# Row terms of the attention scores computed once as a row, from high and low parts, and added to the turned maxima

## What is computed

```python
cq = jnp.einsum('bcd,bqd,d->bcq', c, q, w_cq) + b_cq
s = (c @ w_c + b_c)[:, :, None] + (q @ w_q + b_q)[:, None, :] + cq
a = jax.nn.softmax(s, axis=2)
c2q_att = jnp.einsum('bcq,bqd->bcd', a, q)
b_att = jax.nn.softmax(jnp.max(s, axis=2), axis=1)
q2c_att = jnp.einsum('bc,bcd->bd', b_att, c)[:, None, :]
x = jnp.concatenate([c, c2q_att, c * c2q_att, c * q2c_att], axis=-1)
z = x @ W_l.T + b_l
```

## Time and profile before

| | us |
|---|---|
| median of three runs (430.25 to 432.04) | 431.75 |
| the profiled execution, its own time | 431.75 |
| its span, first to last instruction | 430.1 |
| PE busy in the span | 411.1 |
| DVE busy | 332.1 |
| ACT busy | 214.2 |

### The profile page before, as it was taken

The page is one execution under the profiler, slowest core; times in us unless marked ns, Lnnn a source line. Parts: engine busy times, 40 slices in busy tenths (PEclk is TensorE's granted clock), DMA queues, the critical chain, the costliest instruction groups (busy, mean ns, idle before and its releaser), DMA issues.

```text
span 430.1 us, 8272 instructions
## 1 busy us (share of the span) xinstructions
PE 411.1 (96%) x3090; PEld 313.3 (73%) x3090; DVE 332.1 (77%) x618; ACT 214.2 (50%) x369; POOL 60.1 (14%) x80
## 2 busy tenths in 40 slices
PE   1999999999999999999999979999999999999995
PEld 1566566688898899985568746787777778777783
DVE  4759689966169782449957989899988888988766
ACT  4345225131465343131516333698788887778410
POOL 2130000000432120111102801000000000000152
PEclk9999999999999999999989999999999999999999
DMA  8999697999951450019123579899999999994662
GB/s 291 393 377 360 251 427 307 382 409 407 419 195 26 130 216 2 2 29 414 52 94 154 202 223 366 313 346 375 387 392 379 360 373 381 357 359 197 219 197 98
DMA packets 25006, 116.74 MB, mean 271 GB/s; under 512 B 3286, under 2 KB 3302, under 8 KB 18448
## 3 DMA queue, kind: packets, MB, share of 16 engines
q1 hardware_dynamic: 12448, 92.28, 55.7%
q10 hardware_dynamic: 10448, 19.15, 11.7%
q0 software_dynamic: 2080, 4.90, 3.6%
HBM read 94.04 MB, written 21.23 MB: 268 GB/s over the span
## 4 chain that ended last, share of the span: by engine, by line
PE 82%; DVE 8%; ACT 3%; DMA 2%; POOL 2%; issue 2%; ACTq 0%; DVEq 0%
PE banks L2013 5%; PE banks L2014 5%; PE banks L2015 5%; PE banks L2046 4%; PE banks L1623 4%; PE banks L1627 4%; PE banks L2057 3%; PE banks L2056 3%; PE banks L2055 3%; PE banks L1624 3%; PE banks L1610 3%; PE banks L1664 3%; PE banks L1591 3%; PE banks L1858 3%; PE banks L1734 3%; PE banks L1744 3%
## 5 line engine op out<-in xcount | busy, mean ns | idle before, releaser
L1374 DVE TENSOR_TENSOR w_lo<-w,w_hi 128x1024 fp32r<-128x1024 f32 x48 | 55.5, 1218 | 0.0
L662 ACT ACTIVATE w_hi<-w 128x1024 fp32r<-128x1024 f32 x48 | 47.4, 1095 | 2.4 <-DMA w<-in_w 2.4
L747 ACT ACTIVATE A<-banks,b_sb 128x128 f32<-128x128 f32 x112 | 30.5, 384 | 25.9 <-PE banks L2026 16.4
L2013 PE MATMUL banks<-w_hi,cT_r 128*128 128x512 f32 x100 | 40.1, 401 | 0.0
L2015 PE MATMUL banks<-w_hi,cT_r 128*128 128x512 f32 x100 | 39.0, 390 | 0.0
L2014 PE MATMUL banks<-w_lo,cT_r 128*128 128x512 f32 x100 | 39.0, 390 | 0.0
L1477 DVE COPY A<-banks 128x512 f32<-128x512 f32 x28 | 18.0, 685 | 10.2 <-PE banks L2015 10.2
L858 POOL TENSOR_TENSOR A<-A,hrec 128x1024 f32<-128x1024 f32 x8 | 17.1, 2138 | 61.0 <-DVE hrec L1192 61.0
L900 POOL DMA_DIRECT2D b_sb<-in_b1T x12 | 6.5, 543 | 135.8 <-ACT A L747 120.2
L1623 PE MATMUL banks<-w_lo,A2r 128*128 128x512 f32 x52 | 22.7, 436 | 1.5 <-ACT A2r L529 1.3
L1183 DVE TENSOR_REDUCE hmax<-banks 128x16 f32<-128x1024 f32 x8 | 9.8, 1221 | 18.2 <-PE banks L1809 18.2
(11 more groups left out here) (353 smaller groups left out, 1037.9 us busy)
## 6 DMA issues: line engine op xcount, KB each, us to landing
w<-in_w SPq DMA_DIRECT2D x24, 2048.0 KB, 7.8
rows_dram<-A ACTq DMA_DIRECT2D x1, 14592.0 KB, 50.6
A<-in_ctxT SPq DMA_DIRECT2D x8, 1024.0 KB, 8.8
A<-in_ctx SPq DMA_DIRECT2D x8, 1024.0 KB, 8.6
w<-in_w SPq DMA_DIRECT2D x5, 1024.0 KB, 7.9
w<-in_wlT SPq DMA_DIRECT2D x3, 1024.0 KB, 15.2
wqkv<-in_wqkvT SPq DMA_DIRECT2D x1, 3072.0 KB, 14.9
w<-in_convT SPq DMA_DIRECT2D x1, 3072.0 KB, 13.4
```

The lines of the kernel that those rows point to most:

```text
L662: nc.scalar.activation(w1_hi[:, u, k * F:(k + 1) * F], w1[:, u, k * F:(k + 1) * F], ACT.Copy).then_inc(hi_ready, 1)
L747: ins = nc.scalar.activation(hT[:, u, f, :], HT[f // 4][:, tile(f % 4)], ACT.Gelu, bias=b1_sb[:, u, f:f + 1])
L1374: nc.vector.tensor_tensor(w1_lo[:, u, part], w1[:, u, part], w1_hi[:, u, part].bitcast(F32), ALU.subtract).then_inc(lo_ready, 1)
L2013: mm(HP[u][c][:, :], xr[:, 0, u, k, :], high[:, at], start=(i == 0), stop=False)
```

## The change

The four `row_terms` go. In their place one `row_terms()` has the vector `wc` as stationary operand, and the parts of all four tiles stream past it: for each k three fp32r products, high with high, high with low parts of the tokens, and the vector's low part with the high parts. That is done for tile 0 (128 columns) and for tiles 1 to 3 together (384 columns), 24 instructions in all, and the result is a row in `MI[0:2, 0:512]`. The vector is held twice, so that the stationary operand has two columns. `split_wc` makes its high and low parts on DVE. `take_token_rows` adds the biases and puts the row in SBUF, on storage that another tensor uses later, since `MI` takes other results from then on.

`token_sums` goes. PE now turns `nmax` itself (`turn_maxima`), and DVE's `token_maxima` subtracts the turned row from the stored one in one operation where it had a copy.

The order moves with it. On PE `project_c(2)` stands ahead of `turn_weights(0)`, the new `row_terms()` behind it, `turn_maxima(0)` behind `attend(0)` and `turn_shares(0)` behind `project_c(3)`. On DVE `low_part(0, 3)` moves ahead of `widen(1)`. For the other tiles `turn_maxima(n)` stands where the turn of `msum` stood.

```diff
-        msum = sb("msum", [P, NT])
...
+        wc_hi, wc_lo = sb("wc_hi", [P, KT, 2], F32R), sb("wc_lo", [P, KT, 2], F32R)
...
-        wtmp = sb("wtmp", [P, NT, E]); wselT = sb("wselT", [ROWS3, NT, P], F32R)
-
+        wtmp = sb("wtmp", [P, NT, E]); wselT_f, wselT = overlaid("wselT_f", "wselT", [ROWS3, NT, P])
+
+        token_rows = wselT_f[0:1, :, :].rearrange("o t (j s) -> o t j s", j=2)
...
-            def token_sums(n):
-
-
-                dve.wait_ge(r_psum, n + 1)
-                dve.wait_ge(nmax_ready, n + 1)
-                link(nc.vector.scalar_tensor_tensor(msum[:, n:n + 1], nmax[:, n:n + 1], -1.0, MI[:, 0:1],
-                                                    ALU.mult, ALU.add))
-                nc.vector.tensor_scalar(msum[:, n:n + 1], msum[:, n:n + 1], bsum[:, 0:1], None, ALU.add) \
-                    .then_inc(m_ready, 1)
+            def split_wc():
+
+                dve.wait_ge(score_params_in, 16 * SCORE_PARAMS)
+                twice = wc[:, :].unsqueeze(2).to_broadcast([P, KT, 2])
+                link(nc.vector.tensor_copy(wc_hi[:, :, :], twice))
+                nc.vector.tensor_tensor(wc_lo[:, :, :], twice, wc_hi[:, :, :].bitcast(F32), ALU.subtract).then_inc(wc_parts, 1)
+
+            def take_token_rows():
+
+                dve.wait_ge(r_psum, 1)
+                nc.vector.tensor_scalar(token_rows, MI[0:1, :].rearrange("o (t j s) -> o t j s", t=NT, j=2),
+                                        bsum[0:1, 0:1], None, ALU.add).then_inc(m_ready, 1)
             def token_maxima(n):
                 dve.wait_ge(mT_psum, n + 1)
-                link(nc.vector.tensor_copy(mT[:, :, :], MI[0:1, P:2 * P].rearrange("p (j s) -> p j s", j=2)))
+                dve.wait_ge(m_ready, 1)
+                link(nc.vector.scalar_tensor_tensor(mT[:, :, :], MI[0:1, P:2 * P].rearrange("p (j s) -> p j s", j=2),
+                                                    -1.0, token_rows[:, n], ALU.mult, ALU.add))
...
-            dve.wait_ge(score_params_in, 16 * SCORE_PARAMS)
+            split_wc()
             link(nc.vector.tensor_reduce(bsum[:, :], scal[:, :], AX.X, ALU.add))
-            token_sums(0)
             low_part(0, 2)
+            low_part(0, 3)
             widen(1)
+            take_token_rows()
             token_maxima(0)
-            low_part(0, 3)
             token_shares(0)
...
-            token_sums(1)
...
-                    token_sums(n + 1)
...
-            def row_terms(n):
-
-                if n:
-                    pe.wait_ge(q2c_taken, n)
-                else:
-                    pe.wait_ge(score_params_in, 16 * SCORE_PARAMS)
-                for k in range(KT):
-                    ins = mm(MI[:, 0:1], cT[:, k, tile(n)], wc[:, k:k + 1], start=(k == 0), stop=(k == KT - 1))
+            def row_terms():
+
+                pe.wait_ge(wc_parts, 1)
+                pe.wait_ge(part_high[0], NT)
+                pe.wait_ge(part_low[0], NT)
+                ahead_parts = parts_ahead.rearrange("p t a k n -> p a k t n")
+                for at, high, low in ((tile(0), parts[:, 0, 0], parts[:, 0, 1]),
+                                      (slice(P, N), ahead_parts[:, 0], ahead_parts[:, 1])):
+                    for k in range(KT):
+                        mm(MI[0:2, at], wc_hi[:, k, :], high[:, k], start=(k == 0), stop=False)
+                        mm(MI[0:2, at], wc_hi[:, k, :], low[:, k], start=False, stop=False)
+                        ins = mm(MI[0:2, at], wc_lo[:, k, :], high[:, k], start=False, stop=(k == KT - 1))
                 ins.then_inc(r_psum, 1)
             def turn_weights(n):
...
                 if n:
                     pe.wait_ge(c2qT_ready, n)
                 transposes(TR, att[:, :]).then_inc(aT_psum, 1)
-                pe.wait_ge(m_ready, n + 1)
-                nc.tensor.transpose(MI[0:1, P:2 * P], msum[:, n:n + 1], ident[:, :]).then_inc(mT_psum, 1)
+                if n:
+                    turn_maxima(n)
+
+            def turn_maxima(n):
+
+                pe.wait_ge(m_ready, 1)
+                if n:
+                    pe.wait_ge(q2c_taken, n)
+                nc.tensor.transpose(MI[0:1, P:2 * P], nmax[:, n:n + 1], ident[:, :]).then_inc(mT_psum, 1)
...
             scores(0)
             for n in range(1, NT):
                 turn_normed(0, n)
-            row_terms(0)
             project_c(1)
+            project_c(2)
             turn_weights(0)
-            project_c(2)
+            row_terms()
             attend(0)
+            turn_maxima(0)
+            project_c(3)
             turn_shares(0)
-            project_c(3)
             turn_c2q(0)
             batch_sums(0)
             scores(1)
-            row_terms(1)
...
-                    row_terms(n + 1)
```

More of the change, by code:

```diff
@@ L260, in perceiver_kernel @@
         c2qT_psum, c2qT_ready, cc_ready = map(sem, ("c2qT_psum", "c2qT_ready", "cc_ready"))
-        m_ready, mT_psum, msub_ready, mexp_done = map(sem, ("m_ready", "mT_psum", "msub_ready", "mexp_done"))
+        wc_parts, m_ready, mT_psum, msub_ready, mexp_done = map(sem, ("wc_parts", "m_ready", "mT_psum", "msub_ready", "mexp_done"))
         mn_ready, mn_psum, batt_ready, q2c_psum = map(sem, ("mn_ready", "mn_psum", "batt_ready", "q2c_psum"))
```

## The result

The changed kernel takes 432.9 us (median of 19 runs, 431.79 to 433.58), the kernel before, run beside it, 431.77 us (19 runs, 430.21 to 432.64). The profiled execution took 432.75 us.

The account below looks back on a forecast made before the run. PE was taken to bound the kernel, without idle time from 20.44 to 42.77. 3.1 + 0.2 + 0.85 - 1.9 = +2.25 us on 431.75 gave 434.0 us (forecast 433.2 to 434.8); range 432.0 to 436.3.

Parts of the forecast that it names:

- not slower: Rival: weight pieces start before 36.05, so no 1.8 us wait ahead of part 3; 432.2 us, no change; chance 0.17.
- `attend(0)` later: Tile 0's attention on PE starts when the new row terms end, at 30.6 instead of 27.51: +3.1 us.
- turn of the maxima, and the miss of `batch_sums`: On PE after attend(0): the added turn, and batch_sums(0) missing the copied shares by about 0.1; together 0.2 us.
- the four pieces later: DVE's four pieces of weights, behind the copies of tile 0's shares, start at 37.85 instead of 32.25: 5.6 us later.
- wait ahead of part 3 of tile 0: PE, ready at 42.3, waits until 44.1 for ACT's high part before part 3 of tile 0's projection: 1.8 us.
- tile 1's exponentials wait: Tile 1's exponentials end at 46.6 and PE turns them at 46.9: covered by 0.3 us, so no wait.
- given back by tiles 2 and 3: On PE, the removed row terms of tiles 2 and 3 give back 0.95 us each: 1.9 us.
- sum up to tile 3: All shifts on PE through tile 3: 3.1 + 0.2 + 0.85 - 1.9 = +2.25 us.
- R: Length of the new block of 24 fp32r row-term products on PE: 3.5 us, bounds 2.9 and 4.9.
- The four-fold rate: Rival: the block's 128-column products go at full f32 rate, 0.225 us each; +1.4 us more, 435.4; chance 0.25.
- The clock: Rival: PE's wait halves its clock, doubling the 2.83 us projection behind it; 436.8; chance 0.07, shared with unseen waits.
- carried to the end: Behind the first part all loads and engines hang on PE's progress, so +2.25 us on 431.75 gives 434.0.

Follow-up runs that it names:

- block twice: The changed kernel with its whole block of 24 fp32r row-term products issued twice in a row; 435.73 us, ratio to the kernel before 1.0111.
- before, turns late: The kernel before, own row terms kept, tile 0's sums turned behind attend(0), shares behind project_c(3), low_part(0, 3) moved along on DVE; 432.08 us, ratio 1.0021.
- changed, weights first: The changed kernel with the load of part 1's weights issued ahead of the context of tile 1; 432.41 us, ratio to the kernel before 1.0025.
- changed, reordered: The changed kernel with the product for part 3 ahead of weight pieces 4 and 5 on DVE and ACT; 432.14 us, ratio to the kernel before 1.0021.
- before, reordered: The kernel before with the product for part 3 ahead of weight pieces 4 and 5 on DVE and ACT; 431.15 us, ratio 0.9999.
- on DVE, reordered: The kernel before, tiles 1 to 3's row terms on DVE, vector loaded behind part 3's weights, part 3's product ahead of pieces 4 and 5; 429.25 us, ratio 0.9957.
- on DVE: The kernel before with row terms of tiles 1 to 3 made by multiply and sum on DVE, vector loaded as 256 KB; 429.68 us, ratio 0.9965.
- on DVE, weights first: The kernel before with row terms of tiles 1 to 3 on DVE and the weights of part 1 loaded early; 432.77 us, ratio 1.0031.
- before, weights first: The kernel before with the load of part 1's weights issued ahead of the context of tile 1; 431.12 us, ratio 0.9993.
- before, one row term: The kernel before without the row terms of tiles 1 to 3, tile 0's serving for all four; 429.33 us, ratio 0.9952.
- The changed kernel with pieces early: The changed kernel with weight pieces 2 and 3 moved ahead of take_token_rows on DVE and ahead of exp_maxima(0) on ACT; 432.81 us, ratio to before 1.002.

## Why the prediction was right, and where its size was off

**The number.** The measured 432.9 us lies in the stated range (432.0 to 436.3) but below the forecast proper (433.2 to 434.8, centre 434.0), and it is nearer to the 432.2 of the rival "not slower" than to 434.0. The 0.54 that the kernel would be slower by over 0.5% did not come true either: it is 0.3%. By its number alone the median could not have told the two apart. What decides for the forecast is the trace.

**Direction and mechanism held.** The prediction's steps, counted from `scores(0)`:

| step | forecast | measured |
|---|---|---|
| `project_c(1)` starts earlier | 0.2 | 0.22 |
| `attend(0)` later | 3.1 | 2.48 |
| turn of the maxima, and the miss of `batch_sums` | 0.2 | 0.25 |
| the four pieces later | 5.6 | 4.92 |
| wait ahead of part 3 of tile 0 | 1.8 | 1.61 |
| part 3 of tile 0 later | 4.15 | 3.50 |
| tile 1's exponentials wait | no | no |
| given back by tiles 2 and 3 | 1.9 | 1.74 |
| sum up to tile 3 | 2.25 | 1.79 |

The line of causes is the one foreseen. DVE's timeline in the changed kernel:

```profile
33.01 0.28 DVE L1014 SCALAR_TENSOR_TENSOR mT<-banks,wselT_f 1x128 f32<-1x128 f32 x1 [3.04 <-PE banks L1667]
...
35.92 0.34 DVE L1033 COPY batt<-banks 64x1 f32<-64x1 f32 x2
36.30 4.63 DVE L1053 TENSOR_TENSOR w_lo<-w,w_lo 128x1024 fp32r<-128x1024 f32 x4
...
41.16 0.69 DVE L1069 TENSOR_TENSOR A<-cT,q2cT 128x512 f32<-128x512 f32 x1
...
43.58 0.69 DVE L994 TENSOR_REDUCE nmax<-banks 128x1 f32<-128x512 f32 x1
```

and ACT's:

```profile
41.89 0.63 ACT L530 ACTIVATE A2r<-A 128x512 fp32r<-128x512 f32 x1 [2.70 <-DVE A L1069]
...
44.89 0.19 ACT L536 ACTIVATION_READ_ACCUMULATOR att_f<-banks,nmax 128x1 f32 x1
```

The copies of the shares end at 36.26 and the pieces start at 36.30; product and high part follow, and PE goes on 42.57. Against the earlier trace rows each is late by the same amount. The exponentials end at 45.08 and are turned at 45.43, 0.35 us of cover where 0.3 was forecast.

**The mis-sized term is R.** I had the twelve products of 128 columns at 0.11 us each by the turn of `msum`, the row that I held nearest. The chain of work in the changed kernel:

```profile
26.93 0.06 PE banks L1648
...
27.28 0.17 PE banks L1649
...
29.19 3.58 PE banks L1679 x16
```

They take 0.06, in proportion to their columns like those of 256 and 512, which was my lower bound. The block took 29.12 - 26.15 = 2.97 and not 3.5, 2.9 when issued twice. That is 0.5 of the 0.6 us by which `attend(0)`, the pieces and part 3 came earlier than forecast; put right, the sum is 1.7. The Trainium skill's 81 ns for a pair at 128 columns ("TensorE: Matmul & The Clock Gate", section "Back-to-back issue gap") is nearer than my 0.11 and still above the 0.06 of this trace.

**The rivals.** The four-fold rate fell: 0.06 and not 0.225. "Not slower" fell at its deciding point: it needed the pieces before 36.05 by the prediction's time, 20.56 from the start of `scores(0)`; they started 21.68 from it, and the wait came. The clock did not fall at this wait of 1.61 us: the twelve products behind it took 45.43 - 42.57 = 2.86 us. In the kernel with row terms on DVE and the weights first it did fall, behind 1.99 us of waiting, where the 2.32 us of the earlier trace rows left it up, so that rival was rightly kept.

**The step that the medians do not bear out is "carried to the end" from 431.75.** Between the two profiles it holds: +1.8 less the early start is +0.9, and the spans differ by 1.0. But the medians differ by 1.1 and not by 1.8. What lies between is, as far as known, in the rows of the router. In the kernel before eight f32 products at 216.41 took 5.37 us; windows of the kernel before (columns: window, length, busy us and count of PE, PEld, DVE, ACT and POOL, granted clock, DMA share, GB/s):

```profile
216.00:218.00 2.00, 1.91 (x5) 0.97 (x5) 1.70 (x10) 0.00 (x0) 0.00 (x0) 0.62 0.00 0
218.00:220.00 2.00, 2.00 (x4) 0.80 (x3) 0.44 (x3) 0.00 (x0) 0.00 (x0) 0.52 0.00 0
```

and in PE's timeline of the changed kernel the same eight products, and eight others that took 3.60 us before:

```profile
217.30 3.67 PE L1872 MATMUL banks<-w,cT 128*128 128x512 f32 x8
...
251.44 0.66 PE L1595 MATMUL banks<-ident,A 128*128 128x128 f32 x4 [2.36 <-DMA A<-rows_dram]
251.93 5.29 PE L2052 MATMUL banks<-w,A 128*128 128x512 f32 x8
```

The granted clock of 0.5 to 0.6 is the 1.2 GHz level, for 3.4 of the 4 us by these two figures. Each of the two profiles holds one such stretch, in one of two places, and loses 1.7 us by it (5.37 against 3.67, 5.29 against 3.60); six of the twelve profiled experiments hold none. It shows in the mean granted clock of a run, which every run lists: the eight profiles that hold a stretch have 0.992 to 0.994, the six others 0.997 to 0.999. The values between can't be told apart surely, because in most profiles the clock also falls in the last 2 to 4 us, where PE is done and nothing is lost. Of the 89 runs of the kernel before beside the experiments, 27 had 0.998 or 0.999 and took 430.23 us on average (429.42 to 430.93), 40 had 0.993 or 0.994 and took 431.95 (431.23 to 432.84). Of the changed kernel's 19 runs, which were made earlier, 6 had 0.998 or 0.999, one 0.994, and the other twelve lie between. Runs at 0.998 and 0.999 alone, of every kernel that has any:

| kernel | runs | mean us | less 430.23 | shift up to tile 3 |
|---|---|---|---|---|
| changed | 6 | 432.56 | +2.3 | +1.8 |
| block twice | 1 | 434.95 | +4.7 | +4.7 |
| before, turns late | 4 | 431.10 | +0.9 | +0.9 |
| changed, weights first | 3 | 432.03 | +1.8 | +1.9 |
| changed, reordered | 2 | 431.65 | +1.4 | +1.6 |
| before, reordered | 6 | 430.32 | +0.1 | 0.0 |
| on DVE, reordered | 4 | 428.82 | -1.4 | -0.8 |
| on DVE | 4 | 428.61 | -1.6 | +0.3 |
| on DVE, weights first | 5 | 431.47 | +1.2 | +2.0 |
| before, weights first | 5 | 430.17 | -0.1 | +1.4 |
| before, one row term | 4 | 428.47 | -1.8 | -0.4 |

In the first seven rows the times at one clock follow the traces to 0.6 us, in the last four they do not: they lie 0.8 to 1.9 us below. All four of those profiled executions waited for a late load or behind one, and whether the other runs did is not seen. The change costs about 2 us at one clock: 2.3 at 0.998 and 0.999, and 2.0 if each run of the changed kernel is compared with the runs of before at its own clock. Nearly half of the runs of before are at 0.993 or 0.994 and only one of the changed kernel's, so between the medians only 1.1 us are left. The changed kernel with pieces early is the reverse: ten of its twelve runs had 0.992 to 0.994. Its two at 0.997 took 430.98 us, against 430.71 for the nine of before at that clock, and its four at 0.993 and 0.994 took 432.48 against 431.95, so 0.3 to 0.5 us are left of the change with the wait gone. Its other six, at 0.992, have no run of before beside them. This is the likely reason why its median stayed up.

This sorting was made after the runs, some of its groups are small, and no experiment moved the half-clock stretch on purpose. What decides where and whether it falls is open, and so is whether the change itself makes it rarer. That the clock accounts for the gap between 1.8 and 1.1 is therefore argued from the sorting and not shown by an experiment.

## What to carry to other kernels

Price a replacement by the columns that it streams and by what runs beside it: here four row terms of under 1 us each, of which the first lay beside a wait anyway, became one block of 3 us with nothing beside it, on the engine that is the bound. When a turn is moved behind a long product, follow its consumer's queue on the other engines and not the consumer alone; here a row of 128 numbers held back 4.6 us of weight pieces and with them a high part that PE wanted. And before one profile is set against another, count from a marker ahead of the change and compare the granted clock of the runs: here runs of one kernel at a high and at a low mean clock differ by 1.7 us, more than the medians of the two versions differ.

## What the runs showed of the hardware that was not expected

- An fp32r product of 128 columns with a stationary operand of two columns goes every 0.06 us, one of 384 every 0.17, in proportion. The weight load of each, 0.08 us in its row, adds nothing to this pace.
- PE's clock was at the lower level for about 3.4 us in the router or behind the wait at 252 in some executions and not in others. At 246 to 257 the wait ahead was 2.32 us in one and 2.36 in the other; behind it the same products took 3.60 and 5.29 us.
- Ahead of `scores(0)` fp32r products of 512 columns start every 0.43 us and later every 0.23, while the granted clock of the profile is 1.00 from the start: at the start of the span it does not tell the pace.
- A multiply and sum of 128x512 f32 on DVE takes 0.69 us and 0.08 for reading its sum.
- One load of 1 MB took 13.2 and 15.1 us from issue to landing in two executions of the same kernel.
